# Attention with int8 feed-forward, batch 4: earlier loads for the last phase, fourteen of its periods under the last attention iteration, last heads loaded apart, 1/std by Newton steps on GpSimd

## The reference, cut to what matters

```
h = layernorm(x)
q, k, v = heads(h @ Wq), heads(h @ Wk), heads(h @ Wv)
w = softmax(causal(q @ k.T / 4))                 # per batch and head, 2048 x 2048
x = x + merge(w @ v) @ Wo + bo
h = layernorm(x)
row = max(|h|, 1e-12) / 127 per token ;  col = the same per column of rhs
x = x + (round(h / row) @ round(rhs / col)) * row * col     # integers held in bf16
```

## Time and profile before

| | us |
|---|---|
| median of 3 runs | 1781.94 |
| lowest, highest | 1778.69, 1784.92 |
| the profiled execution: its time | 1783.09 |
| the profiled execution: its span | 1780.5 |

### The profile page before, as it was taken

How to read it: one execution, slowest core, us unless ns; L and a number is a source line. 1 busy time by engine, 2 the same in 40 slices (tenths; PEclk the granted TensorE clock), 3 DMA queues, 4 the chain that set the end, 5 groups by cost and what they waited for, 6 DMA issues and landing times.

```text
span 1780.5 us, 39694 instructions
## 1 busy us (share of the span) xinstructions
PE 1632.9 (92%) x16319; PEld 618.9 (35%) x16319; DVE 1525.9 (86%) x1819; ACT 1368.7 (77%) x2618; POOL 324.3 (18%) x371
## 2 busy tenths in 40 slices
PE   6999989999999999999999999999999999699964
PEld 4455443333333333333333333333333333234442
DVE  4677769999999989899999999999999999267877
ACT  2233349898888888888989898989888888488842
POOL 5333300111111111111010101010111111224442
PEclk9999999999999999999999999999999999799886
DMA  3443310101010111111111111010101010455442
GB/s 111 136 136 120 108 61 16 48 17 47 17 47 26 39 32 32 33 32 32 32 42 37 34 32 44 20 48 17 48 17 47 17 47 14 144 152 164 119 149 71
DMA packets 102991, 106.12 MB, mean 60 GB/s; under 512 B 19608, under 2 KB 86428, under 8 KB 102812
## 3 DMA queue, kind: packets, MB, share of 16 engines
q1 hardware_dynamic: 102812, 103.60, 19.4%
HBM read 60.56 MB, written 42.47 MB: 58 GB/s over the span
## 4 chain that ended last, share of the span: by engine, by line
PE 39%; DVE 34%; ACT 8%; issue 2%; DMA 1%; SPq 1%; POOL 0%; POOLq 0%; ACTq 0%; DVEq 0%
DVE pmax L400 29%; PE psum L1037 16%; PE psum L1017 10%; PE psum L308 6%; ACT prob L1199 6%; PE psum L322 2%; PE psum L327 2%; DVE pblk L400 2%; PE psum L1074 2%; DMA out<-V 1%; DVE V L1343 1%; ACT L1199 1%; ACT L1171 1%; DMA f_x<-in_L_attn_x 1%; PE psum L1098 0%
## 5 line engine op out<-in xcount | busy, mean ns | idle before, releaser
L1199 ACT ACTIVATE prob<-psum 128x512 f32<-128x512 f32 (+1 forms) x2304 | 1193.8, 573 | 178.0 <-PE psum L1017 146.5
L400 DVE TENSOR_REDUCE pmax<-psum 128x2 f32<-128x1024 f32 (+1 forms) x960 | 1107.0, 1214 | 70.6 <-PE psum L308 33.5
L1037 PE MATMUL psum<-prob,V 128*32 128x256 f32 x8704 | 697.3, 393 | 0.0
L1017 PE MATMUL psum<-Q,K 50*128 50x512 f16 (+3 forms) x2560 | 434.4, 351 | 41.7 <-ACT prob L1199 34.7
L1238 POOL TENSOR_SCALAR_AFFINE_SELECT prob<-prob 128x512 f32<-128x512 f32 x256 | 159.4, 634 | 1181.5 <-ACT prob L1199 1181.4
L308 PE MATMUL psum<-K,Q 48*128 48x512 f16 x1536 | 293.3, 385 | 17.5 <-DVE pmax L400 17.5
L1037 PEld LDWEIGHTS psum<-prob,V 128*32 128x32 f32 x8704 | 171.9, 108 | 280.4 <-issue 217.1
L1017 PEld LDWEIGHTS psum<-Q,K 50*128 50x128 f16 x2560 | 119.1, 93 | 259.4 <-ACT prob L1199 208.6
L308 PEld LDWEIGHTS psum<-K,Q 48*128 48x128 f16 x1536 | 71.0, 92 | 311.8 <-DVE pmax L400 170.4
L400 DVE TENSOR_REDUCE pblk<-psum 128x8 f32<-128x1024 f32 x128 | 152.3, 1215 | 2.3 <-PE psum L327 1.3
L327 PE MATMUL psum<-K,Q 48*128 48x512 f16 (+3 forms) x1024 | 126.2, 299 | 0.0
(11 more groups left out here) (106 smaller groups left out, 737.4 us busy)
## 6 DMA issues: line engine op xcount, KB each, us to landing
f_x<-in_L_attn_x SPq DMA_DIRECT2D x32, 512.0 KB, 3.7
unnormalised<-ust SPq DMA_DIRECT2D x64, 256.0 KB, 3.1
q_parts<-part SPq DMA_DIRECT2D x64, 128.0 KB
k_parts<-part SPq DMA_DIRECT2D x64, 128.0 KB
Q<-q_parts SPq DMA_DIRECT2D x128, 64.0 KB, 2.4
K<-k_parts SPq DMA_DIRECT2D x128, 64.0 KB, 2.0
f_us<-unnormalised SPq DMA_DIRECT2D x32, 256.0 KB
f_rs<-inverse_sums SPq DMA_DIRECT2D x32, 256.0 KB
```

The lines of the kernel that those rows point to most:

```text
L400: nc.vector.tensor_reduce(to, of, axis=AX.X, op=ALU.max).then_inc(M.mx_free, 1)
L1017: m = nc.tensor.matmul(PS[:, SB + (i + half) % RING, at:at + n], K[it % 2][rows, pair, kb * P:(kb + 1) * P], Q[it % 2][rows, pair, (c + 1) ...
L1037: m = nc.tensor.matmul(PS[32 * h:32 * h + 32, UB, to:to + n], V[:, it // NG * NT + kb, col:col + 32], prob[(it * NSTEP + k) % PRING][:, h, ...
L1199: nc.scalar.activation(prob[g % PRING][:, h, 0:n], PS[:, SB + i % RING, 0:n], ACT.Exp, scale=by).then_inc(exp_done, 1)
```

## The change

- Blocks 0 to 3 are loaded one iteration earlier: one block behind each of the four chunks of iteration 13. The bias is prepared and sent one iteration earlier as well.
- Fourteen periods (`UNDER` = 14) lie under the last iteration: 84 units over 72 half steps, by `units_at`, so some half steps issue two. The second part of the preparation of the feed-forward weight comes at step 2, not 3.
- For blocks 0 to 12 (`LATE` = 13) 1/std is not Sqrt on ScalarE and a reciprocal. VectorE computes var + eps, a first guess from its bits, and -0.5 times it (three small operations, `first_guess`, right behind `variance`). GpSimd does three Newton steps of four operations on 128x4 each, every one waiting for the one before (`newton_step`). `normalise` waits for the last.
- GpSimd's order in periods under 12 is `divide`, Newton, `residual`; from period 12 on Newton, `residual`, `divide`; the divides of blocks 14 and 15 come last.
- `residual` of blocks 11 to 15 (`ADDED` = 11) is done by VectorE, behind `scaled`.
- Blocks 12 to 15: u and inverses of 12 heads, and x, are loaded as for other blocks, three periods ahead. Only the last group's 4 heads wait for the last iteration (`last_group`, two DMAs). The sums come in four pieces. SyncE's order in periods 8 to 13 changes: storing results and fetching sums stands behind `store`. VectorE inverts a piece at the head of periods 9, 12 and 14, and the last one behind `variance` in period 14.
- Behind the iteration TensorE does `transpose` and `ffn` first in a period, then the four quarters; VectorE takes `scaled` and `residual` first.

```diff
-UNITS, DELAY = 6, 3
-UNDER = 2 * NSTEP // UNITS
+UNITS, DELAY, UNDER = 6, 3, 14
+LATE, ADDED = 13, 11
+INSIDE, BEHIND = (0, 1, 2, 3, 4, 5), (1, 5, 0, 2, 3, 4)
+def units_at(half):
+    first, last = (n * UNDER * UNITS // (2 * NSTEP) for n in (half, half + 1))
+    return [(n // UNITS, n % UNITS) for n in range(first, last)]
+def load_heads(sp, F, u_d, r_d, j, o, first, heads):
+    s, b, c = j % 4, ORDER[j] // NCH, ORDER[j] % NCH
+    rows = slice(first * DH, (first + heads) * DH)
+    src = slice(b * H + o * (P // DH) + first, b * H + o * (P // DH) + first + heads)
+    sp.dma_start(F.us[s][rows, o, :], u_d[src, 0:DH, c * CH:(c + 1) * CH]).then_inc(F.x_in[s], 16)
+    inverses = r_d[src, c * CH:(c + 1) * CH].unsqueeze(1).to_broadcast([heads, DH, CH])
+    sp.dma_start(F.rs[s][rows, o, :], inverses).then_inc(F.x_in[s], 16)
...
# SyncE
+                    if it == ITS - 3:
+                        load_last_phase(sp, F, x_t, u_d, r_d, ci)
-                    if ci == 2 and it == ITS - 2:
+                    if it == ITS - 2 and ci == 0:
                         sp.wait_ge(bo_parts, 8)
...
-                        sp.wait_ge(r_stored, (ITS - 2) * 16)
-                        for j in range(4):
-                            load_last_phase(sp, F, x_t, u_d, r_d, j)
...
             for p in range(1, PERIODS):
+                if p == 4:
+                    inverses_from(ITS - 2)
+                if 4 <= p + 3 < NC:
+                    if p + 3 == NC - NCH:
+                        sp.wait_ge(r_stored, (ITS - 1) * 16)
                     load(p + 3)
+                if p in (9, 12):
+                    last_inverses(p // 12)
+                if p in (10, 12):
+                    last_group(p // 12)
                 if 0 <= p - DELAY - 1 < NC:
                     store(p - DELAY - 1)
+                if p in (8, 11):
+                    store_results(ITS - 1, p // 11)
+                    last_sums(p // 11)
+                if p == 13:
+                    for i in (2, 3):
+                        store_results(ITS - 1, i)
+                        last_sums(i)
+                    for i in (2, 3):
+                        last_inverses(i)
+                        last_group(i)
...
# GpSimd
+            def newton_step(j, step, last):
+                done = 4 * (3 * j + step)
+                y = guess[j % 2]
+                pool.wait_ge(newton, done)
+                nc.gpsimd.tensor_tensor(nsq, y, y, ALU.mult).then_inc(newton, 1)
+                pool.wait_ge(newton, done + 1)
+                nc.gpsimd.tensor_tensor(nfac, nsq, mhalf[j % 2], ALU.mult).then_inc(newton, 1)
+                pool.wait_ge(newton, done + 2)
+                nc.gpsimd.tensor_scalar(nfac, nfac, 1.5, None, ALU.add).then_inc(newton, 1)
+                pool.wait_ge(newton, done + 3)
+                nc.gpsimd.tensor_tensor(rstd[j % 4][:] if last else y, y, nfac, ALU.mult).then_inc(newton, 1)
+            def one_over_std(j):
+                pool.wait_ge(guess_ready, 2 * j + 2)
+                for step in range(3):
+                    newton_step(j, step, step == 2)
             def unit(p, third):
-                if third == 0 and p + 1 < NC:
+                if third == (0 if p < NC - NCH else 2) and p + 1 < UNDER:
                     divide(p + 1)
-                if third == 1 and 0 <= p - DELAY - 1 < NC:
+                if third == 2 and p == UNDER:
+                    divide(UNDER)
+                    divide(UNDER + 1)
+                if third == (1 if p < NC - NCH else 0) and 0 <= p - 1 < LATE:
+                    one_over_std(p - 1)
+                if third == (2 if p < NC - NCH else 1) and 0 <= p - DELAY - 1 < ADDED:
                     residual(p - DELAY - 1)
...
# VectorE
+            def first_guess(j):
+                v = var[j % 2]
+                dve.wait_ge(var_ready, j + 1)
+                if j >= 2:
+                    dve.wait_ge(newton, 12 * (j - 1))
+                nc.vector.tensor_scalar(v, mv[j % 2][:, :, 1], EPS, None, ALU.add).then_inc(v_ready, 1)
+                dve.wait_ge(v_ready, j + 1)
+                nc.vector.tensor_scalar(guess[j % 2].bitcast(I32), v.bitcast(I32), -0.5, ROOT_BITS, ALU.mult,
+                                        ALU.add).then_inc(guess_ready, 1)
+                nc.vector.tensor_scalar(mhalf[j % 2], v, -0.5, None, ALU.mult).then_inc(guess_ready, 1)
             def normalise(j):
-                dve.wait_ge(rstd_ready, j + 1)
+                if j < LATE:
+                    dve.wait_ge(newton, 12 * (j + 1))
+                else:
+                    dve.wait_ge(rstd_ready, j - LATE + 1)
...
```

More of the change, by code:

```diff
@@ L847, in attend @@
         tmp = [in_values([TPC, D]) for s in range(2)]
-        stats = [sb(f"f_stats{s}", [P, TPC, 6]) for s in range(2)]
-        mv = [sb(f"f_mv{s}", [P, TPC, 2]) for s in range(2)]
-        std = [sb(f"f_std{s}", [P, TPC]) for s in range(2)]
+        stats = [in_values([TPC, 6]) for s in range(2)]
+        mv = [in_values([TPC, 2]) for s in range(2)]
+        std, var, mhalf, guess = ([in_values([1, TPC])[:, 0, :] for s in range(2)] for _ in range(4))
+        nsq, nfac = in_values([1, TPC])[:, 0, :], in_values([1, TPC])[:, 0, :]
         rstd, amax, rowscale, rowinv = ([sb(f"f_{name}{s}", [P, TPC]) for s in range(4)] for name in
@@ L1137, in _ @@
             for p in range(UNDER, PERIODS):
-                for u in range(UNITS):
+                for u in BEHIND:
                     unit(p, u)
@@ L1201, in _ @@
                         if h % 2 == 1 and it + 1 == ITS:
-                            unit((2 * k + h // 2) // UNITS, (2 * k + h // 2) % UNITS)
+                            for p, u in units_at(2 * k + h // 2):
+                                unit(p, u)
             take(ITS - 1, NCH - 1)
             for p in range(UNDER, PERIODS):
-                for u in range(UNITS):
+                for u in (0, 1, 3, 2):
                     unit(p, u)
@@ L1231, in _ @@
                     if it + 1 == ITS:
-                        unit(k // 3, k % 3)
+                        for n in range(k * 3 * UNDER // NSTEP, (k + 1) * 3 * UNDER // NSTEP):
+                            unit(n // 3, n % 3)
                     if parts[0][0] < TPC * c:
@@ L1370, in _, with take_integers @@
             dve.wait_ge(p_free, (ITS - NG) * NSTEP)
-            for p in range(1, PERIODS):
+            def take_integers(p):
+                if 0 <= p - DELAY - 1 < NC:
+                    scaled(p - DELAY - 1, 0)
+                    scaled(p - DELAY - 1, 1)
+                    if p - DELAY - 1 >= ADDED:
+                        residual(p - DELAY - 1)
+            for p in range(1, PERIODS):
+                if p > UNDER:
+                    take_integers(p)
+                if p in (2, 9, 12):
+                    if p == 2:
+                        invert(ITS - 2)
+                    else:
+                        last_invert(p // 12)
+                if p == UNDER:
+                    last_invert(2)
                 if p - 1 < NC:
```

106 lines of the change are left out of this document (45 added, 61 removed).

## The result

The changed kernel takes 1788.62 us in the median of 8 runs (1787.46 to 1790.05), the kernel before 1780.51 (1778.69 to 1784.92) beside it. The ratio is 1.0044 [1.0034, 1.0055]: slower by 0.44%, 8 us, where 1770 was forecast. The profiled execution has a span of 1785.7 us, 5.2 more than before.

What follows compares the result with a forecast made beforehand. No engine was taken as full; gaps at the last iteration's start and behind it, and ScalarE's root with table loads, cost time. 1571.4 + 133 + 6 = 1710.4, plus 57 = 1767.4, plus 2.6: 1770 us, range 1752 to 1794.

Steps and rivals of the forecast that it cites:

- the start is gained: Start of the last iteration: with blocks 0 to 3 loaded earlier, TensorE starts block 0 at 1530.0 instead of 1541.75, 11.7 us.
- t(1): Start of `add_x` in VectorE's period 1: forecast 8.6 us after TensorE's block 0, at 1538.6, 15.5 us sooner.
- t(4): Start of `add_x` in period 4: forecast at 1571.4, against 1592.2 before, after three periods without `residual` on GpSimd.
- the price of an operation: Each small Newton operation on GpSimd: 0.2 to 0.5 us possible, 0.3 taken, so 3.6 us for twelve.
- t(p): Start of `add_x`, which opens VectorE's period p; Newton's chain was forecast to end 7.9 us after it.
- The lock's place: SBUF port shared by VectorE and GpSimd: `residual` starts as Newton ends and holds `normalise` for 2.35 us.
- From t(4) to t(14) ten periods: 133 us: Ten periods under the last iteration, from period 4's `add_x` to period 14's, at 13.3 us each.
- waits for sums in periods 9 and 12: Heads of these periods, where VectorE inverts sums fetched late by SyncE: 3 us each, 6 in all, bounds 0 and 6 each.
- wait for sums ahead of t(14), and the end: From `add_x` of period 14 to the end of the span: 57 us, with the third chunk's sums 4.4 us late.
- the rival C: GpSimd's next `divide` takes the port again and `normalise` waits twice: 15.7 us a period, 1794 us; chance 0.13.
- a rival that the prediction gave a chance of 0.05: TensorE's granted clock falls to 0.65 in half of the periods: +10 us, 1780, no change; chance 0.05.
- ScalarE loses 2.87 us ... no longer a bound: Periods under the last iteration: ScalarE is freed of the root (0.30 us) and its two table loads (1.28 each).

## Why the prediction was wrong

**Right: that the start is gained.** TensorE's block 0 was put at 1530.0 and came at 1528.15, with the whole iteration 1.9 us earlier. The loads alone are worth 12 us by experiment. One term was mis-sized: from there to t(1) were 12.0 us, not 8.6. A shorter idle was to shorten the slow stretch; behind 2.33 us of idle the granted clock was 0.50 all the same, and a quarter of `out_proj` took 2.07 us. That t(4) came at 1573.47 against 1571.4 is in part luck: the 3.4 us were offset by the 1.9 of the earlier iteration.

**Right: the price of an operation.** 0.28 to 0.30 us from start to start against 0.3; the guess is out 3.6 us behind t(p); the chain ends 7.3 to 8.7 us behind t(p) in eight of periods 4 to 12, and at 9.75 in period 5. The lock's place was as worked out in five of the nine periods, and its size there was 2.0 us against 2.35. The Trainium skill ("SBUF — State Buffer", SBUF: two separate sides) has the lock as exclusive for a whole instruction, and this trace agrees: the held operation ends 0.15 us behind the GpSimd one, and four operations take 3.39 us, 1.38 alone.

**Wrong: "From t(4) to t(14) ten periods: 133 us".** Without the waits for sums they took 146.7. Two steps of the prediction fail here: period 13 was taken to be one like the others, and a period was put at 13.3 us. The account of the span, 18.3 us above 1767.4:

| step | predicted | measured | us |
|---|---|---|---|
| t(4) | 1571.4 | 1573.47 | +2.1 |
| periods 4 to 12, without waits for sums | 9 x 13.3 = 119.7 | 127.5 | +7.8 |
| period 13, without the wait for sums | 13.3 | 19.2 | +5.9 |
| waits for sums in periods 9 and 12 | 6 | 7.2 | +1.2 |
| wait for sums ahead of t(14), and the end | 57 | 5.7 + 52.6 | +1.3 |

The row of period 13 is a step that was missing. The prediction saw that SyncE's list delays the sums and sized that rightly (3 each, measured 3.90 and 3.32). It didn't follow the same list one entry further, to block 13's last heads, whose inverse store stands behind block 15's five DMAs: 7.7 us of TensorE standing. Moving them and the sums in SyncE's list gives 13.0 us of time; the waits in the table (7.2) and the surplus of period 13 (5.9) are 13.1.

The row of the nine periods is a term mis-sized, 14.2 us in place of 13.3. Period 5 alone has 3.8 of its 7.8 us: the rival C, once, with `residual` and `divide` one behind the other beside `normalise`, and a chain that ended 1.9 us late, because two masks stood ahead of it on GpSimd. It did not come again as the rival's rule would have it: in periods 4, 7, 8, 10 and 11 `normalise` pays the single lock of 2.0 us, as forecast, in period 12 2.9, and in 6 and 9 none. In period 6 the lock fell on `integers` (2.88 us in place of 0.69), and `normalise` started only at 10.1. In period 9 VectorE instead waits 3.38 us at the end, for a `residual` that GpSimd did only behind its masks. The rest, 4.0 us, is spread over the other eight. TensorE's granted clock stands beside it, a rival that the prediction gave a chance of 0.05: 0.87 from t(4) to t(13), between 0.64 and 0.81 in periods 6, 7, 9 and 12. With Newton on the better SyncE order TensorE is busy 107.53 us in nine periods at 0.92, with the root 100.22 at 1.00, for the same 790 matmul records. So 7.3 of the 17.2 us between those two kernels are the same matmuls taking longer. TensorE waits more for `add_x` there (20.2 us from 1524 to 1740 against 3.8), so the lower clock goes with those waits; how much of the 17.2 would be there at a full clock was not separated, and stays open.

**What the sum could not show: what Newton costs.** The prediction's period of 13.3 was as long as that of the kernel before, and so Newton seemed to cost nothing. This is not a term of the sum that failed, but it is why the change as a whole loses. The comparison that counts is fourteen periods with the root on ScalarE, 12.3 us each. "ScalarE loses 2.87 us ... no longer a bound" is true and buys nothing: with the root ScalarE had 96.89 of 110.60 us to do there, so it was not full. VectorE did wait for it, 9.3 us in the nine periods, 2.6 of them for the root; with Newton, on the same order of SyncE, it waited 4.2 for ScalarE and 9.9 for the chain. By the Trainium skill ("ScalarE: Activation LUTs", What ACT_TABLE_LOAD costs) a switch costs about 2.66 us, twice the row's 1.28; no period of these traces shows that. ScalarE's root is ready before VectorE is through `integers` in six of nine periods, Newton's chain in three. Removing work from an engine with slack in exchange for a longer chain on the path is what costs 11.9 us (14.5 in twelve periods). With early loads at 12 gained, Newton 11.9 lost and SyncE's order 13 lost, and the rest of the change (two more periods under the iteration, `residual` behind it on VectorE, last heads apart) at some 5 to 6 gained (1768.08 against 1762.29), the sum is a loss of 7 to 8, and 8 were measured. The last term is itself a difference of these runs, so the sum only says that the two losses add up within 1.4 us; the three parts in it were not separated.

Of the twelve expectations only three ended in a stated range: the early loads, SyncE's order, and order and root together. Five were out by 0.4 to 2.6 us (the root, `residual` on VectorE, the later inversions, all of `residual` with the root, Newton with twelve periods), Newton behind `scaled` by 3.2. Newton on VectorE, one Newton step and `residual` first were out by 7 to 21 us. The first and the last of these, and Newton behind `scaled`, I put down to one fault: I looked at how long one engine's list is, and not at who waits for the entries behind the changed one. With one Newton step I had undervalued the length of the chain.

## What to carry to other kernels

Price a move of work against the kernel that has the rest of the change without it, not against the kernel before: a step that seems free may eat what another gives. In lists that are worked off in order, follow every entry behind an inserted or delayed one to whoever waits for it, DMA queue included; an 8 KB store behind a block's five loads held up its reader for 7.4 us, ahead of them for 2.1. Before taking work off an engine, see whether its chain was shorter there than it will be on the other.

## What the runs showed of the hardware

- Small operations on 128x4: 0.20 us on GpSimd, 0.28 to 0.30 from start to start when each waits for the one before; 0.16 to 0.17 on VectorE, 0.20 from start to start.
- The lock also holds up the smallest VectorE operation: a scale on 128x4 took 2.17 us instead of 0.17 beside `divide`. A `tensor_tensor` on 128x4 took 2.35 us instead of 0.16 beside `residual` (Newton on VectorE behind `scaled`, at 1622.22). Four operations of `normalise` took 5.73 us instead of 1.38 beside two GpSimd operations in a row: each of the two held one of them.
- A store of 8 KB behind five DMAs on SyncE's queue held up the load that waited for it 7.4 us from the end of its issue; ahead of them it was 2.1 us.
- TensorE's granted clock was 0.50 for 4.35 us behind 2.33 us of idle, and 0.51 for 4.3 us behind 14.03 us.
